# Expert weights prepared in the head, mixing weights carried in the rows, the last attention unit in another order

## The reference

```python
x = x + proj(attention(theta x, phi x, values x))   # 4 images, 128 channels, 32 x 32; f / sqrt(64), softmax
t = to_tokens(x)                                    # 4 x 1024 tokens of 128
t = t + attention(layernorm(t), Wk, bk, Wq, bq, Wv, bv)          # softmax(q k / sqrt(128)) v
xf = layernorm(t).reshape(-1, 128)                  # 4096 tokens
top_w, top_i = top_k(xf @ Wg + bg, 2); top_w = softmax(top_w)    # 2 of 8 experts per token
for e in range(8):
    h = gelu(xf @ W1[e] + b1[e])                    # 128 -> 512, erf gelu
    out = out + w_dense[:, e:e+1] * (h @ W2[e] + b2[e])          # 512 -> 128
x = from_tokens(t + out)
```

## Time and profile before

| | us |
|---|---|
| median of 3 runs (lowest, highest) | 491.48 (490.86, 491.91) |
| the profiled execution: its own time | 489.35 |
| its span, first to last instruction | 487.6 |
| busy in it: PE, DVE, ACT, POOL | 389.0, 370.3, 335.2, 313.0 |
| mean granted TensorE clock, of full speed | 0.939 |

### The profile page before, as it was taken

One profiled execution on the slowest core, in us unless ns is written; L12 is line 12 of the kernel. 1 busy time (PEld: TensorE's weight loads), 2 busy tenths in 40 slices (PEclk: granted clock), 3 DMA queues, 4 the chain that ended last, 5 costly groups with the idle time before them and its releaser, 6 DMA issues.

```text
span 487.6 us, 12633 instructions
## 1 busy us (share of the span) xinstructions
PE 389.0 (80%) x3948; PEld 291.9 (60%) x3949; DVE 370.3 (76%) x1012; ACT 335.2 (69%) x636; POOL 313.0 (64%) x309
## 2 busy tenths in 40 slices
PE   2666669999988799989987876658989999999552
PEld 1433337666665466666655644646879898989321
DVE  2577989998897787889898588667976666666863
ACT  3635887778785499876756875558778787888320
POOL 9200132755699856598857857767777777777780
PEclk9988999999998999999999989778999999999955
DMA  6750000610000000000510101133355333334717
GB/s 216 169 93 0 1 0 3 151 25 3 1 1 0 2 1 1 1 1 2 137 38 12 31 27 40 51 88 94 91 127 132 105 101 93 98 94 113 225 49 258
DMA packets 43836, 32.62 MB, mean 67 GB/s; under 512 B 17686, under 2 KB 36905, under 8 KB 43785
## 3 DMA queue, kind: packets, MB, share of 16 engines
q1 hardware_dynamic: 39242, 22.59, 19.0%
q0 software_dynamic: 4544, 9.38, 5.8%
HBM read 18.33 MB, written 13.60 MB: 65 GB/s over the span
## 4 chain that ended last, share of the span: by engine, by line
PE 41%; DVE 31%; ACT 10%; issue 8%; POOL 6%; DMA 2%; SPq 1%; ACTq 0%; POOLq 0%; DVEq 0%
PE MX L696 13%; PE PV L696 11%; PE SC L696 11%; DVE mx L1519 6%; DVE EL L1542 5%; PE PR L696 4%; POOL ybuf L685 3%; ACT EH L1168 2%; ACT E L1167 2%; ACT QK L1076 2%; DVE QK L1493 2%; DVE EH L1738 1%; ACT X L1076 1%; PE PR L965 1%; DVE TOK L1561 1%
## 5 line engine op out<-in xcount | busy, mean ns | idle before, releaser
L1167 ACT ACTIVATE E<-SC 128x512 f32<-128x512 f32 x128 | 77.2, 603 | 43.4 <-PE SC L696 36.5
L696 PE MATMUL PV<-VH,EH 128*128 128x129 f16 x512 | 96.0, 227 | 3.0 <-DVE TOK L1561 3.0
L696 PE MATMUL SC<-QK 128*128 128x512 f16 x320 | 90.6, 389 | 8.2 <-ACT EH L1168 6.1
L618 POOL TENSOR_TENSOR EL<-E,EH 128x1024 f32 (+1 forms) x28 | 59.6, 2128 | 56.7 <-ACT EH L1168 56.7
L696 PE MATMUL PV<-VH,EL 128*128 128x129 f16 x512 | 95.6, 225 | 0.0
L696 PE MATMUL PV<-VL,EH 128*128 128x128 f16 x512 | 95.6, 223 | 0.0
L1519 DVE TENSOR_REDUCE mx<-MX 128x1 f32<-128x1024 f32 x64 | 78.0, 1219 | 18.8 <-PE MX L696 18.5
L685 POOL DMA_INDIRECT ybuf<-EL,yid x62 | 70.0, 1130 | 18.9 <-issue 17.4
L569 POOL DMA_INDIRECT zbuf<-ZZ,posi x64 | 66.4, 1038 | 21.3 <-issue 18.2
L1168 ACT ACTIVATE EH<-SC 128x512 f32 (+1 forms) x128 | 77.6, 606 | 0.0
L696 PE MATMUL MX<-QK,EH 128*128 x624 | 62.2, 246 | 1.9 <-DVE EL L1749 1.9
(11 more groups left out here) (231 smaller groups left out, 886.8 us busy)
## 6 DMA issues: line engine op xcount, KB each, us to landing
EH<-zbuf SPq DMA_DIRECT2D x39, 130.0 KB, 2.4
X<-in_x_dram SPq DMA_DIRECT2D x4, 512.0 KB, 5.1
zbuf<-zer SPq DMA_DIRECT2D x16, 128.0 KB, 4.0
X<-in_L_ffn_W_dram SPq DMA_DIRECT2D x1, 2048.0 KB
EL<-ybuf SPq DMA_DIRECT2D x4, 512.0 KB, 4.2
out_dram<-X SPq DMA_DIRECT2D x8, 256.0 KB, 4.8
W1H<-in_L_ffn_W_dram SPq DMA_DIRECT2D x4, 256.0 KB
W1L<-in_L_ffn_W_dram SPq DMA_DIRECT2D x4, 256.0 KB
```

Of the source, the lines that this page charges most:

```text
L618: nc.gpsimd.tensor_tensor(EL[:, w % 2, ds(i * 2, 2), c], E32h[1], EH[:, w % 2, ds(i * 2, 2), c], ALU.subtract).then_inc(e32_free[1], 1)
L696: return nc.tensor.matmul(o, w, r, start=start, stop=stop)
L1167: nc.scalar.activation(E32h[h][:, p, :], SC[:, p, :], ACT.Exp, scale=sc)
```

## The change

Five things are altered.

1. W1, its row 0 broadcast to the other partitions, and b1 are loaded right behind the gate's weights, into `EL1` and `EH1`, which units 0 and 1 leave free at first. GpSimd's four subtractions and four low halves of W1 move ahead of its first step; ACT's eight scaled copies from step 4 to step -1, a quarter behind each pair, each quarter waiting for one subtraction. DVE waits in step 1 for the low halves. The transfers that preset unused tiles come later, W2's load moves from unit 7 to unit 2.
2. In steps -2 and -1 ACT makes the fp16 copy of the image before the copy of the residual stream, and in step -1 the row maxima alternate between `SC` and `MX` rather than using `MX` alone.
3. A row becomes 264 16-bit words, moved as 132 32-bit words; the two new ones hold the token's two mixing weights for images 0 to 2 (1.0 and 1.0 for image 3). ACT makes the exponentials per image, DVE the weights (`weigh`) ahead of `place`. A tile's result is multiplied by its row's weight: two small operations make `share`, and two `tensor_scalar` of 128x128 take the place of the reduction. For that the output is summed wholly in PSUM: 26 products of 128 columns for the 8 of 256 and 10 of 128. At the end images 0 to 2 are added by 12 operations of 128x512, image 3 is mixed as before (16 operations).
4. In step 8, image 2's logits, tops and picks come ahead of the second pair on DVE, `place` ahead of the third, and the table of the first 8 tiles moves from step 7 to behind that `place`. On PE the pairs' output products are interleaved with logits and rank accordingly. In step 9 ACT copies tile 0's transposed rows before it normalises, and PE makes tile 0's hidden products ahead of the last four transposes.
5. In step 7 GpSimd issues the scatters of image 1 as soon as it may, four of them between two `split_last`.

```diff
-ROW = 2 * P + 4
+ROW = 2 * P + 8
@@ SyncE, head
+            sp.dma_start(W1w.rearrange("p (e h) -> p e h", e=E), W1.rearrange("e d h -> d e h")).then_inc(w1_in, 16)
+            for e in range(E):
+                sp.dma_start(W10b[e // PAIRS][1:P, e % PAIRS * HID:(e % PAIRS + 1) * HID],
+                             W1[e, 0, :].partition_broadcast(P - 1)).then_inc(w1_row_in, 16)
@@ GpSimd, ahead of the steps (removed from s == 3 and s == 5)
+            pool.wait_ge(w1_zeroed, 2)
+            pool.wait_ge(w1_row_in, 16 * E)
+            pool.wait_ge(w1_in, 32)
+            for i in range(PAIRS):
+                c = slice(i * S, (i + 1) * S)
+                nc.gpsimd.tensor_tensor(W1w[:, c], W1w[:, c], W10b[i // 2][:, i % 2 * S:(i % 2 + 1) * S],
+                                        ALU.subtract).then_inc(w1_augmented, 1)
+            for i in range(PAIRS):
+                pool.wait_ge(wexp_scaled, i + 1)
+                c = slice(i * S, (i + 1) * S)
+                nc.gpsimd.tensor_tensor(W1L[:, c], W1w[:, c], W1H[:, c], ALU.subtract).then_inc(wexp_lo, 1)
@@ GpSimd, s == 7
                     pair(0, before)
-                    for i in range(PAIRS - 1):
-                        scatter(IN_UNIT * (i + 1), IN_UNIT)
-                        split_last(i)
-            for b in range(1, B):
+                    scatter(IN_UNIT, IN_UNIT)
+                    split_last(0)
+                    scatter(2 * IN_UNIT, 2 * IN_UNIT)
+                    split_last(1)
+                    pool.wait_ge(rows_ready, 2)
+                    scatter(2 * T, IN_UNIT)
+                    split_last(2)
+            scatter(2 * T + IN_UNIT, 2 * T - IN_UNIT)
+            for b in range(2, B):
@@ PE, row maxima
-                    pe.wait_ge(mx_free, i * 2 + (n_mx + p + 1))
+                    if s == -1:
+                        pe.wait_ge(mx_free, i * 2 + (n_mx + p) if p else i * 2 + n_mx)
+                    ...
+                    o_ = first_maxima[p] if s == -1 else MX
@@ PE, s == 8
                     rows_whole()
-                    pair(1, False, second=True)
+                    outputs(1, 0)
                     logits_whole()
-                    pair(2, False, rest=True)
+                    outputs(1, 1)
+                    pe.wait_ge(e32_free[1], PAIRS * (a + 1) + 1)
+                    outputs(2, 0)
                     rank(2)
+                    outputs(2, 1)
                     pair(3, False, rest=True)
@@ PE, output of a tile, of each half q
-                        if c < HC - 1:
-                            mm(o_, hh[:, b % 2, k], both[c], c == 0, False)
-                            mm(o_[:, 0:P], hl[:, b % 2, k], both[c][:, :, 0, :], False, False)
-                        else:
-                            ...
+                        mm(o_, hh[:, b % 2, k], both[c][:, :, 0, :], c == 0, False)
+                        mm(o_, hl[:, b % 2, k], both[c][:, :, 0, :], False, False)
+                        if c == HC - 1:
+                            mm(o_, mine, B2[:], False, False)
+                        last = mm(o_, hh[:, b % 2, k], both[c][:, :, 1, :], False, c == HC - 1)
@@ ACT, step -1 (removed from s == 4)
-                    if s == 4:
+                    if s == -1:
                         first_weights(i)
@@ DVE, s == 8
                     last_unit_pair(0)
-                    last_unit_pair(1)
                     logits_whole()
                     tops(2)
                     picks(2)
+                    last_unit_pair(1)
+                    weigh(2)
+                    place(2)
+                    full_tiles(0, FIRST)
                     last_unit_pair(2)
-                    place(2)
                     last_unit_pair(3)
@@ DVE, output of a tile
+                link(nc.vector.scalar_tensor_tensor(out=share[:, j % 2, :], in0=words[:, :, 1], ...))
+                link(nc.vector.tensor_tensor(share[:, j % 2, :], share[:, j % 2, :], parts[:, :, 1], ALU.max))
                 dve.wait_ge(y_full, j + 1)
-                nc.vector.reduce_sum(y32[b], sums, AX.X).then_inc(y_ready, 1)
+                for q in range(2):
+                    at = (j % 2) * HALF + q * P
+                    last = nc.vector.tensor_scalar(y32[b][:, q, :], MX[:, at:at + P], share[:, j % 2, q:q + 1], None,
+                                                   ALU.mult)
+                last.then_inc(y_ready, 1)
@@ DVE, the end, images 0 to 2
+            def add_halves(k):
+                ...
+                dve.wait_ge(y_in[k], 16)
+                link(nc.vector.tensor_tensor(TOK[:, t, :], TOK[:, t, :], yin[k // 2][:, at, 0, :], ALU.add))
+                link(nc.vector.tensor_tensor(TOK[:, t, :], TOK[:, t, :], yin[k // 2][:, at, 1, :], ALU.add))
+                nc.vector.memset(spare[:], 0.0).then_inc(summed, PAIRS)
```

More of the change, by code:

```diff
@@ L871, in pair @@
                     late = late_pair(u, a, i)
+                    if first and u == 0:
+                        pe.wait_ge(mx_free, n_mx)
                     if first and u is not None:
@@ L1179, in _, with gaps @@
                 routed = v is not None and v >= UNITS and not whole(v)
+                def gaps(c):
+                    act.wait_ge(gap_ready, c + 1)
+                    nc.scalar.activation(egap[:, T * c:T * c + T], gap[:, c, :], ACT.Exp).then_inc(egap_ready, 1)
                 def pair(i, before, first=False):
@@ L1193, in pair @@
                         exponentials(u, i, 1, 0)
+                    if routed and i == 2:
+                        gaps(v - UNITS)
                     if before is not None:
@@ L1402, in picks, with weigh @@
                 nc.vector.tensor_tensor(picked[:], hot[:, 0], hot[:, 1], ALU.add).then_inc(picked_ready, 1)
-            def weigh():
-                dve.wait_ge(egap_ready, 1)
-                link(nc.vector.tensor_scalar(den[:], egap[:], 1.0, WS, ALU.add, ALU.mult))
-                link(nc.vector.reciprocal(WT[:, 0, :], den[:]))
-                link(nc.vector.tensor_tensor(WT[:, 1, :], egap[:], WT[:, 0, :], ALU.mult))
+            def weigh(c):
+                dve.wait_ge(egap_ready, c + 1)
+                t = slice(T * c, T * c + T)
+                first, second = (ZW[:, t, q] if c < B - 1 else WT[:, q, :] for q in range(2))
+                link(nc.vector.tensor_scalar(den[:, t], egap[:, t], 1.0, WS, ALU.add, ALU.mult))
+                link(nc.vector.reciprocal(first, den[:, t]))
+                link(nc.vector.tensor_tensor(second, egap[:, t], first, ALU.mult))
             def place(c):
@@ L1766, in mixes @@
-            def mixes(ns):
-                tiles_ = sorted(set(n // 2 for n in ns))
-                for half in range(2):
-                    for t in tiles_:
-                        mix(2 * t + half)
+                parts = words[:, :, 2:4].bitcast(F32)
+                link(nc.vector.scalar_tensor_tensor(out=share[:, j % 2, :], in0=words[:, :, 1],
+                                                    scalar=tabf[:, 1, j:j + 1], in1=parts[:, :, 0], op0=ALU.is_equal,
+                                                    op1=ALU.mult))
@@ new lines, in mix @@
+            def mix(k):
+                dve.wait_ge(y_in[2 * (B - 1) + k], 16)
+                for half in range(2):
+                    for i in (2 * k, 2 * k + 1):
+                        t = (B - 1) * T + i
+                        if half:
+                            dve.wait_ge(mixed, i + 1)
+                        nc.vector.scalar_tensor_tensor(out=TOK[:, t, :], in0=yin[B - 1][:, i, half, :],
+                                                       scalar=WT[:, half, i:i + 1], in1=TOK[:, t, :], op0=ALU.mult,
+                                                       op1=ALU.add).then_inc(summed if half else mixed, 1)
```

152 lines of the change are left out of this document (67 added, 85 removed).

## The result

The changed kernel takes 557.28 us (median of 4 runs, 556.88 to 558.08) where the kernel before takes 491.17. It is 66 us slower, far outside the range of 471.5 to 487. The profiled execution has a span of 555.9 us, 68.3 more than before.

What follows compares the result with a forecast made beforehand. No engine was taken to bound the whole (PE 41% of the chain, DVE 31%). Terms -8.2 + 2.0 + 1.2 + 0.5 - 9.4 = -13.9 us took the median 491.48 to 477.6, range 471.5 to 487.

Steps and rivals of the forecast that it cites:

- the head's price of the row-0 broadcasts: Before step 0: 2 MB of broadcasts at 169 GB/s, 12.3 us or a little less, landing near 28.5.
- The prediction's own sign: Stated in advance: the prediction is wrong if ACT's wait in the head is longer than 8 us.
- rival C: Head: broadcasts land at 32.5, step 0 starts 6 us later and not 2, time 481.6; chance 0.12.
- Steps 3 to 5: Attention steps relieved of W1 work on GpSimd and ACT: -8.2 us together, bounds -5 and -11.4.
- rival D: Steps 3 to 5 keep their length through another wait; half of the 8.2 us comes, time 481.7; chance 0.15.
- The head with the shape mended: Up to step 0's first exponential: start near 44 where before 42.39, taken as +2.0 us, bounds -1.5 and +6.
- Weighing: Steps 6 and 7: weights of images 0 and 1 on DVE, 0.6 us each, +1.2, bounds 0 and +2.
- Step 8: Reordered work around image 2's places and the first table: +0.5 us on the chain, between -2.5 and +2.
- Tiles: Tile loop: eight more products per tile, +0.05 us a tile at most, +1.4 over 39 tiles.
- Rival B: Tile loop gets issue-bound on PE's 26 products: slower from +0.39 us a tile, up to 501; chance 0.10.
- End: Last puts pass between DVE's additions, two behind the last result; landing 9.4 us earlier, tiles' 2.1 included.
- Rival A: End: last puts stay locked out until DVE's additions finish; gain 2.6 instead of 9.4, time 484.4; chance 0.15.

Runs made afterwards that it cites:

- f_split: The changed kernel with each row-0 broadcast cut into 112 and 15 partitions, on a chip where the kernel before took 489.05 us: 481.79 us, ratio 0.986.
- e1_split112: The changed kernel with each row-0 broadcast cut into 112 and 15 partitions, on a slow chip: 580.36 us against 572.35 of the kernel before there, ratio 1.019.
- u_no45: The changed kernel with broadcasts cut into 112 and 15 partitions, without parts 4 and 5: 481.35 us, ratio 0.984 to the kernel before.

## Why the prediction was wrong

- **The step that failed** is the head's price of the row-0 broadcasts: "the second slice, in which the same row-0 broadcasts ran, moved at 169 GB/s", and so "the broadcasts, 2 MB more, 12.3 us later or a little less". They were not the same broadcasts: `[:]` and `P` had become `[1:P]` and `P - 1`. I priced bytes by a rate that belongs to another shape. At 25 GB/s eight of 254 KB take 83 us and not 12.3. GpSimd's first subtraction began at 103.43, written was 28.5, and step 0 began at 120.25, written was 44; this was the +78. The prediction's own sign, ACT's wait in the head over 8 us, showed it with 82.4. The fall-back, rival C, had the right place and a price of 4 us.
- **Steps 3 to 5**: forecast -8.2, measured -10.5, within the bounds. The steps came down to PE's busy time plus 0.5 to 1.6 us, so rival D fell. Step 3 went beyond its own bound (-7.2, where -6.7 was the most): I took PE's 30.1 us of busy time as fixed, but it had been made at a granted clock of 0.95, and at 1.00 it was 27.96. Rival D's "29.3" of DVE in step 3 stands in no row; it is 29.2.
- **The head with the shape mended**: forecast 44, measured 44.55 (f_split) and 45.48 (e1_split112). In f_split GpSimd began its subtractions at 27.73; written was 28.5.
- **Weighing**: forecast +1.2 for two steps; step 6 alone took +3.5. The operations took 1.05 us in the step and not 0.6, and lengthened it by 0.9 where the clock held (u_no45); the other 2.4 us and more are PE's half clock, which the sum did not have. It came in six of seven profiles with the weighing and in two of seven without.
- **Step 8**: +0.5 forecast; without parts 4 and 5 the time is the same within what can be told, as u_no45 shows.
- **Tiles**: forecast +1.4, measured +4.5 from the third to the last. The pace a tile was right: +0.02, nearer to what the Trainium skill's formula gives (VectorE: DVE Perf Modes, The TRN2 errata: +0.02, my estimate from it 0.8 us for 39) than to my 0.05. The turns of the loop were not thought of. Rival B's +0.39 a tile did not come.
- **End**: forecast -9.4 with +2.1 of tiles inside, so -11.5 behind the last result; measured -9.8. I had two puts behind the last result and the landing 5.3 us behind it; there were three, the last began at 463.55 in f_split and had landed 2.94 us later, 7.0 behind the last result at 459.53. I had also counted the 2.23 us of landing from the put's end, where the chain counts it from its start. Rival A is refuted: beside additions of 0.69 us no put of the changed kernel or of f_split took over 1.26 us. Nor did none wait: those puts took 0.15 to 0.29 us longer than 0.97.
- **The range** is also a little off from its own terms: gains at their bounds in steps 3 to 5 and the head are 3.2 and 3.5 us more than the forecast's, which gives 470.9 and not 471.5, and A and C, or D and A, reach 488.4 or 488.5. This changes nothing in the outcome.

Without the broadcasts' form the sign would have been right and the size not: f_split gained 7.3 us where 13.9 were forecast, for step 6, the tiles and the end. With them it had the wrong sign. The chance of 0.08 for slower stood wholly on PE's products, while no chance stood on the one transfer whose form was new.

## What to carry to other kernels

When a diff changes the partition range of a transfer, price its shape first, then its bytes: 127 partitions moved at 25 GB/s here and 124 at 99, while with pieces of 112 and 15 everything was in by 29 us. If partition 0 must be spared, cut the rest in two pieces, or write it too and mend it afterwards.

Before a long DVE row of operations with two SBUF inputs gets between GpSimd and its last transfers, open gaps in it with waits, but only for as long as the transfers last: each gap cost 0.12 us, and sixteen of them gained 5.6 us.

Read the granted clock of a step before its growth is laid to the edit: of the 3.3 us here, 0.9 were the added work and the rest a half clock, which came in most profiles with that work, not in all, and in some without it. Likewise, PE's busy time is a floor only at the clock at which it was measured: 30.1 us in step 3 became 27.96.

## What was not expected of the hardware

- Transfers on one DMA engine also held up the issuing queue: the first two broadcasts were issued in 8.6 us together, but each of the other six took SyncE 10.4 to 10.5 us instead of about 0.5, and so did the 0.5 KB transfer behind them.
- Between chips the same kernel differed by 17%: 489.05 us on one and 572.35 on another. Of the slow chip only changed versions were profiled; in the part with the tiles much of ACT's waiting is put down to nothing on this core ("remote", 77.5 us in e1_split112). The attention steps 1 to 6 of e1_split112 and f_split, the same kernel, agree within 0.3 us each. Its cause is open.
- `tensor_tensor` with both inputs in SBUF holds a put back too: 1.12 to 1.26 us beside linked additions, 0.97 elsewhere.
